# First output-projection chunk inside the attention's last groups, broadcasts behind the scores, and no embedding table: two attention layers in float32

## The reference, cut to what matters

```
x: 2 x 512 x 48 x 48, 8 heads of 64, 2304 tokens per image
layer 0: xn = group_norm(x, 32 groups) * w + b
         q, k, v = qkv_w @ xn + qkv_b
         a = softmax(q k^T / 8) v              (per image and head)
         x = proj_w @ a + proj_b + x
layer 1: emb = 32 rows that depend on the image row h, 32 on its column w
         q, k = [x, emb] @ Wq, [x, emb] @ Wk ; v = x @ Wv
         o = softmax(q k^T / 8) v
         out = o @ Wout + bout + x
```

## Time and profile before

| | us |
|---|---|
| median of 3 runs (4218.84 to 4219.61) | 4218.99 |
| the profiled execution's own time | 4219.53 |
| its span | 4217.8 |
| PE (TensorE) busy | 4099.4, 97% |
| DVE (VectorE) busy | 3278.0, 78% |
| ACT (ScalarE) busy | 2763.7, 66% |
| POOL (GpSimd) busy | 1773.6, 42% |
| waits of PE for ACT before L661, 92 times | 22.6 |

### The profile page before, as it was taken

The page is one execution under the profiler, slowest core; times in us unless marked ns, Lnnn a source line. Parts: engine busy times, 40 slices in busy tenths (PEclk is TensorE's granted clock), DMA queues, the critical chain, the costliest instruction groups (busy, mean ns, idle before and its releaser), DMA issues. The chain is left out here.

```text
span 4217.8 us, 88347 instructions
## 1 busy us (share of the span) xinstructions
PE 4099.4 (97%) x30024; PEld 1901.6 (45%) x30024; DVE 3278.0 (78%) x4032; ACT 2763.7 (66%) x3557; POOL 1773.6 (42%) x572
## 2 busy tenths in 40 slices
PE   7999999999999999998999989999999999999989
PEld 4554344444444444444555544444444444444445
DVE  3111999999999999997322239999999999999962
ACT  1112888888888888886000018888888888888840
POOL 0000455555555555553100005555555555555520
PEclk9999999999999999999999999999999999999999
DMA  4112000101000000011333220101000000000116
GB/s 176 75 75 94 10 27 19 37 13 32 20 28 22 22 23 26 26 49 51 118 102 127 97 95 9 31 20 32 19 28 24 22 22 26 24 21 30 42 47 215
DMA packets 157932, 208.41 MB, mean 49 GB/s; under 512 B 9008, under 2 KB 144304, under 8 KB 156848
## 3 DMA queue, kind: packets, MB, share of 16 engines
q1 hardware_dynamic: 137712, 179.28, 12.9%
q10 hardware_dynamic: 20160, 28.32, 1.8%
HBM read 113.19 MB, written 94.37 MB: 49 GB/s over the span
## 5 line engine op out<-in xcount | busy, mean ns | idle before, releaser
L589 POOL TENSOR_TENSOR prob<-prob,mx 128x1056 f32<-128x1056 f32 x564 | 1752.6, 3107 | 2237.0 <-DVE prob L589 2237.0
L753 ACT ACTIVATE prob<-psum_att 128x768 f32<-128x768 f32 x1728 | 1353.9, 822 | 938.6 <-PE psum_att L684 535.4
L684 PE MATMUL psum_att<-qst,kst 64*128 64x384 f32 x6912 | 1286.2, 504 | 30.3 <-DMA kst<-qk_scratch 17.8
L769 ACT ACTIVATE prob<-prob 128x1152 f32<-128x1152 f32 x1152 | 1292.9, 1175 | 16.5 <-POOL prob L589 14.5
L695 PE MATMUL psum_att<-prob,vst 128*32 128x384 f32 x13824 | 1239.3, 490 | 0.4 <-issue 0.4
L856 DVE TENSOR_TENSOR run<-psum_att,run 128x768 f32<-128x768 f32 x1152 | 1057.8, 947 | 24.3 <-PE psum_att L684 23.1
L589 DVE TENSOR_TENSOR prob<-prob,mx 128x1248 f32<-128x1248 f32 (+1 forms) x576 | 972.1, 1688 | 0.0
L684 PEld LDWEIGHTS psum_att<-qst,kst 64*128 64x128 f32 x6912 | 621.9, 187 | 575.2 <-issue 174.2
L695 PEld LDWEIGHTS psum_att<-prob,vst 128*32 128x32 f32 x13824 | 393.7, 109 | 718.4 <-issue 529.1
L870 DVE TENSOR_TENSOR two_tiles<-prob 128x768 f32<-128x768 f32 x564 | 534.4, 948 | 0.0
L309 PE MATMUL psum<-xc_l,wq 128*128 128x384 f32 x1536 | 504.0, 489 | 9.9 <-DVE qk_l L406 4.8
(11 more groups left out here) (56 smaller groups left out, 1690.9 us busy)
## 6 DMA issues: line engine op xcount, KB each, us to landing
qk_scratch<-qk_l SPq DMA_DIRECT2D x48, 768.0 KB, 3.5
v_scratch<-vo_l SPq DMA_DIRECT2D x24, 768.0 KB, 3.5
qst<-qk_scratch SPq DMA_DIRECT2D x96, 192.0 KB, 2.4
kst<-qk_scratch SPq DMA_DIRECT2D x96, 192.0 KB, 2.4
vst<-v_scratch SPq DMA_DIRECT2D x96, 192.0 KB, 2.5
att_scratch<-ob ACTq DMA_DIRECT2D x96, 192.0 KB, 1.9
attc_l<-att_scratch SPq DMA_DIRECT2D x24, 768.0 KB, 5.4
x_sb<-in_x SPq DMA_DIRECT2D x8, 1152.0 KB, 14.0
```

The lines of the kernel that those rows point to most:

```text
L589: return engine.tensor_tensor(x, x, m, ALU.subtract)
L684: mm = nc.tensor.matmul(psum[:, 2 * k + e, 0:CH], kst[rows, (3 * c + k) * P:(3 * c + k + 1) * P], qst[par][rows, :], start=True, stop=True ...
L753: nc.scalar.activation(prob[par][:, :, s, :], s_banks(k)[:, :, 0:CH], ACT.Copy).then_inc(copied, 1)
L769: nc.scalar.activation(x, x, ACT.Exp, scale=SCALE).then_inc(exp_done, 1)
```

## The change

- The broadcasts of the maximum come behind the scores of group 1, and signal once per pair of banks; VectorE's maxima of group 1 and ScalarE's copies of the maximum wait for them one by one. `spread_den` waits per bank.
- VectorE's share of the shift of group 3 is 304 columns, of the others 208.
- At t = 48, groups 2 and 3, and t = 50, groups 2 and 3, TensorE does one tile each of the next stage's chunk 0 output projection, in banks 0 to 3. In those last bodies the denominators go to banks 4 and 5. The next stage's VectorE reads chunk 0 from there; its TensorE begins with the next thing.
- In layer 1 no table is made: row parts are added as a tile leaves PSUM, column parts in a second, in-place addition in SBUF. TensorE waits for the first addition alone.
- Each tile of x is loaded in two halves, with a semaphore for each.

```diff
-SHIFT_DVE = 208
+XH = 2
+SHIFT_DVE = [208, 208, 208, 304, 208, 208]
+OUT_AHEAD = {(0, 2): (0,), (0, 3): (1,), (2, 2): (2,), (2, 3): (3,)}
@@ first_norm_stage, load_x
-                sp.dma_start(gn["x"][:, c, b * HW:(b + 1) * HW],
-                             x_d[c * P:(c + 1) * P, b * HW:(b + 1) * HW]).then_inc(gn["x_in"][n], 16)
+                for h in range(XH):
+                    tokens = slice(b * HW + h * HW // XH, b * HW + (h + 1) * HW // XH)
+                    sp.dma_start(gn["x"][:, c, tokens], x_d[c * P:(c + 1) * P, tokens]).then_inc(gn["x_in"][n][h], 16)
@@ qkv_stage, TensorE
+            if out_proj:
+                pe.wait_ge(w_in[out_proj["w_at"]], 16)
+                pe.sem_inc(out_mm, CT)
...
-                out_tiles(0, 0)
-                            pe.wait_ge(qk_out, MT * i + m - 3)
+                            pe.wait_ge(qk_read, MT * i + m - 3)
@@ qkv_stage, VectorE
+            def add_cols(i, m):
+                half, mt = divmod(m, CT)
+                dve.wait_ge(qk_read, MT * i + m + 1)
+                nc.vector.tensor_tensor(image(qk[half][:, mt, :]), image(qk[half][:, mt, :]), emb_cols(m), ALU.add)\
+                    .then_inc(qk_out, 1)
...
-                            nc.vector.tensor_tensor(qk[half][:, mt, :], qk_bank(m), emb_of(i, m), ALU.add)\
-                                .then_inc(qk_out, 1)
+                            nc.vector.tensor_tensor(image(qk[half][:, mt, :]), image(qk_bank(m)), emb_rows(i, m),
+                                                    ALU.add).then_inc(qk_read, 1)
+                            if m > 0:
+                                add_cols(i, m - 1)
+                            if m == MT - 1:
+                                add_cols(i, m)
@@ output_stage, TensorE
+                    if is_block(i, 0):
+                        pe.wait_ge(early["out_mm"], CT)
+                        pe.sem_inc(out_mm, CT)
+                        continue
@@ attention_stage, TensorE
-                mm.then_inc(broadcast, 1)
+                    mm.then_inc(broadcast, 1)
...
+                    bank_free(t + 3, DEN_SPREAD_AT, r)
+                    mm = nc.tensor.transpose(spread_part(t, r), dwide[:, r, :], ident)
...
+            def first_out_tiles(tiles):
+                pe.wait_ge(ahead["w_in"], 16)
+                pe.wait_ge(ahead["att_in"], 16)
+                for m in tiles:
+                    w = [ahead["w"][:, c, m * P:(m + 1) * P] for c in range(CT)]
+                    out_projection(nc, psum[:, m, 0:CH], w, ahead["att"]).then_inc(ahead["out_mm"], 1)
...
-                    if c == BROADCAST_AT and not before(t, 1) and live(t - 1):
-                        broadcast_max(t - 1, c)
...
                     if c == TURN_AT and not before(t, 1) and live(t - 1):
                         bank_free(t, c, 2)
                         turn(t - 1)
+                    if c == BROADCAST_AT and not before(t, 1) and live(t - 1):
+                        broadcast_max(t - 1, c)
                     tv, pv, cv = behind(t, par, c, PV_LAG)
                     if live(tv):
                         weigh(tv, pv, cv)
+                    if not live(t) and (t - NB, c) in OUT_AHEAD:
+                        bank_free(t, c, 2)
+                        first_out_tiles(OUT_AHEAD[t - NB, c])
+                    if live(tv):
                         add_keys(tv, pv, cv)
@@ attention_stage, ScalarE, copy_max
-                    act.wait_ge(broadcast, t + 1)
+                act.wait_ge(broadcast, 3 * t + r + 1)
@@ attention_stage, VectorE, maximum
+                if s // 3 == BROADCAST_AT and not before(t, 1):
+                    dve.wait_ge(broadcast, 3 * (t - 1) + s % 3 + 1)
```

More of the change, by code:

```diff
@@ L53, in norm_buffers @@
         gn[name + "_sem"] = ctx.enter_context(nc.semaphore(name))
-    gn["x_in"] = [ctx.enter_context(nc.semaphore(f"x_in{n}")) for n in range(N)]
+    gn["x_in"] = [[ctx.enter_context(nc.semaphore(f"x_in{n}_{h}")) for h in range(XH)] for n in range(N)]
     return gn
@@ L223, in pairs_of_chunks, with image, emb_rows, emb_cols @@
             pair(NCH // 2 - 1, True)
[L225 to L229, removed]
+        def image(x):
+            return x.rearrange("p (h w) -> p h w", w=SIDE)
+        def emb_rows(i, m):
+            return bufs["emb_parts"][:, m, bass.ds(i % JB * (CH // SIDE), CH // SIDE)].unsqueeze(2)\
+                .broadcast_to([P, CH // SIDE, SIDE])
+        def emb_cols(m):
+            return bufs["emb_parts"][:, m, SIDE:2 * SIDE].unsqueeze(1).broadcast_to([P, CH // SIDE, SIDE])
         @block.sync
@@ L511, in _, with attention_stage @@
                 pair(it)
-def attention_stage(nc, name, psum, bufs, qk_d, v_d, att_d, next_loads):
+def attention_stage(nc, name, psum, bufs, qk_d, v_d, att_d, next_loads, ahead):
     with ExitStack() as ctx:
@@ L755, in copy_max @@
             def copy_max(t, par, r):
-                if r == 0:
-                    act.wait_ge(broadcast, t + 1)
-                    if not before(t, 2):
-                        act.wait_ge(dve_shifted, group(t - 2, KC - 1))
-                        act.wait_ge(pool_shifted, group(t - 2, KC - 1))
+                act.wait_ge(broadcast, 3 * t + r + 1)
+                if r == 0 and not before(t, 2):
+                    act.wait_ge(dve_shifted, group(t - 2, KC - 1))
+                    act.wait_ge(pool_shifted, group(t - 2, KC - 1))
                 nc.scalar.activation(mx[par][:, :, r * P:(r + 1) * P], s_banks(r)[:, :, CH:512], ACT.Copy)\
@@ L841, in reduce @@
                 if not before(t, 1):
-                    dve.wait_ge(broadcast, t)
+                    dve.wait_ge(broadcast, 3 * t)
                 nc.vector.tensor_reduce(mcol[:, :, r], s_banks(r)[:, :, CH:512], AX.X, ALU.max).then_inc(reduced, 1)
@@ L876, in shift @@
                 dve.wait_ge(copied, slot(t, 3 * c + 2))
[L877 removed]
+                shift_part(nc.vector, par, c, 0, CH if last(t) else SHIFT_DVE[c]).then_inc(dve_shifted, 1)
             def sum_den(t, k):
@@ L969, in early_loads @@
                      "res": sb_(c1, nc, f"resc0_{stage}", [P, CT, CH])}
-            for signal in ("w_in", "att_in", "res_in"):
+            for signal in ("w_in", "att_in", "res_in", "out_mm"):
                 early[signal] = c1.enter_context(nc.semaphore(f"{signal}_{stage}"))
@@ L974, in early_loads, with attention @@
                            (early["res"][:, :, :], rows(res_d, 0), early["res_in"])]
-        def attention(layer, next_loads):
+        def attention(layer, next_loads, ahead):
             with ExitStack() as c2:
-                psum = c2.enter_context(nc.psum_tensor(f"psum_att{layer}", [P, 8, 512], F32))
                 def two(name, shape, dt=F32):
@@ L991, in attention @@
                         "ones": ones, "ident": ident}
-                attention_stage(nc, f"att{layer}", psum, bufs, qk_d, v_d, att_d, next_loads)
+                attention_stage(nc, f"att{layer}", psum, bufs, qk_d, v_d, att_d, next_loads, ahead)
         def semaphores(c1, stage, n):
@@ L1015, in program @@
             we_in, em_in, wq_in, wv_in = semaphores(c1, "l1", 4)
-            attention(0, [(we[:, :], w1e, we_in), (em[:, :], emb, em_in)] + loads)
+            attention(0, [(we[:, :], w1e, we_in), (em[:, :], emb, em_in)] + loads, early)
             wq = sb_(c1, nc, "wq1", [P, CT, 2 * C])
```

61 lines of the change are left out of this document (24 added, 37 removed).

## The result

Changed kernel: 4226.97 us (4225.29 to 4228.74, 19 runs); kernel before, same chips: 4219.6 us (4218.4 to 4221.3, 19 runs). Ratio 1.0018, 95% interval [1.0011, 1.0024]: slower by 0.18%, where 4175.6 was forecast. The profiled execution's span goes from 4217.8 to 4224.0, +6.3 us; forecast was -43.4, so 49.7 us have to be explained. The steady block's period is 32.48 us (32.26 before, 31.98 forecast), and 86 of them make 43 of the 49.7. Two of the prediction's own signs of being wrong have come: a period above 32.1, and PE waiting elsewhere in the block.

The account below looks back on a forecast made before the run. Bound: a steady-block loop closed by DVE and PE, with three ACT copies between. Gains 24.9 + 1.7 + 1.7 + 10.4 + 3.4 + 1.3 = 43.4 us lead from 4219.5 to 4176.1, median 4175.6; range 4154 to 4205.

Parts of the forecast that it names:

- signs of being wrong: Steady block: wrong if the period is above 32.1 or below 31.8, or if PE waits elsewhere in the block.
- The two idles vanish: Steady block: DVE's two 0.25 us idles, waiting for PE's scores of groups 3 and 4, disappear.
- no stall left, none to spare: Group 1's second and third score tiles: PE reaches each 0.15 us after its copy, just enough for the semaphore.
- The steady sum: Steady block, loop through DVE: 3.71 + 9.74 + 5.29 + 12.67 + 0.57 = 31.98 us, 0.29 less than now.
- the forecast's loop over PE: Steady block: PE between groups 1 and 4 (15.67 becomes 16.34), DVE after it; 31.78 us in all.
- The hold-up: DVE's shift behind the reductions, held up 1.25 us by GpSimd's shift (2.70 against 1.45); 1.1 to 1.25 of it goes.
- PE takes over: Rival, steady block: DVE starts its maximum sooner, period falls to 31.68 to 31.78, time 4154; chance 0.20.
- the hold-up stays: Rival, steady block: GpSimd's time does not go with its columns, period 32.34, time 4210 or 4203; chance 0.16.
- Slower: Rival, group 1: PE holds the first score until the last copy, period 33.38, time 4299; chance 0.05.
- Tails and seams: Attention ends and next stages: each attention ends 2.3 us later; layer 1 gains 10.4, the output stage 3.4.
- The tail gives nothing: Rival, attention tails: the four tiles cost there what they save behind, 7 us of the seams go, 4183; chance 0.09.
- Start: Kernel start: with x in halves only three statistics remain behind the last load; gain 1.3 us, between 0 and 1.4.

Follow-up runs that it names:

- x2: Changed kernel with the denominator's transposes (`turn_den`) moved between group 3's second and third score tiles: 4195.94 us, 0.9948.
- e1: Changed kernel with VectorE's share of the group 3 shift back at 208 columns: 4218.86 us, 0.9998.
- y1: x4 with output tiles 2 and 3 moved from in front of the last denominator to the start of the next stage: 4179.46 us, 0.9903.
- x4: x2 with the shift at 208 columns everywhere: 4187.61 us, 0.9925; run a second time, 4188.42 us.
- x1: e3 with chunk 0's output projection back in its own stage, no tiles ahead: 4198.12 us, 0.9948.
- e3: Changed kernel with both the shift at 208 columns and the broadcasts back ahead of the scores: 4197.63 us, 0.9946.
- x3: e3 with only the last pair of broadcasts put behind the first score tile: 4192.91 us, 0.9937.
- e4: Changed kernel with each pair of broadcasts directly behind its own score tile, 304 columns kept: 4218.08 us, 0.9995.

## Why the prediction was wrong, step by step
**The failed step** is "The two idles vanish since PE, starting group 1 earlier, is 0.2 to 0.3 ahead there". I walked the loop that goes through DVE alone, and the one through PE from group 1 to 4; not the one that leaves PE at the broadcast and returns to it at `turn_den`. In the trace after, it adds up:
- PE from group 3's scores (1510.54) to the next group 1 (1531.24), without idle time: 20.70
- scores and broadcast to DVE's first maximum, 1498.75 to 1501.65: 2.90
- maxima of groups 1 and 2, to 1506.49 + 2.68 = 1509.17: 7.52
- ScalarE's third copy, to 1510.01: 0.84
- `turn_den`, 1510.01 to 1510.54: 0.53

That is 32.49. A sum round a closed loop always gives the period; what shows that this path holds the block is that its links follow on each other without slack, and x2, which takes one link out. DVE's shift of group 3 and its reductions are not in it. They are in a second loop that passes `turn_den` too: from group 3's scores over DVE's work to the reductions (DVE idles only 0.19 and 0.09 in it, for PE), then over ScalarE's copies to the third score tile of group 1. That one is longer by the 0.11 of e1, and it is what the tiles wait for; with 208 columns the first loop is left. The same sum in e1, where the scores take 2.14 and not 2.25, is 32.39 (measured 32.37). The trace of the kernel before was enough to see it. Counted from the start of group 1's scores on PE, `turn_den` was reached after 1504.66 - 1494.96 = 9.70 us and its bank was free after 1504.55 - 1494.96 = 9.59. The new order puts 0.80 of broadcast into the first path, and into the second the difference of the first maximum's start, 2.61 forecast against 1496.20 - 1494.96 = 1.24, so 1.37. From 0.11 early the bank becomes 0.46 late, and with 0.05 from ScalarE to PE that is a wait of 0.51; measured is 0.52. In PE's list of waits it was missing because it was hidden by 0.11.

A second step was too small: "no stall left, none to spare" for the score tiles. PE started group 1 0.10 sooner than forecast and then waited for copies two and three, 0.11 in group 1, and 0.10 for the third tile of group 2. Seen from PE the changed block is 31.67 + 0.59 at `turn_den` + 0.11 + 0.10 = 32.47; the block before was 31.67 + 0.44 + 0.15 = 32.26.

**The steady sum, term by term.** From the first reduction's end to the first maximum, 3.71 forecast, 3.90 measured (PE starts after 1.00 in place of 1.10, but scores take 2.25 in place of 2.13, and from the first broadcast to DVE it takes 0.65 in place of 0.48). The idles before groups 3 and 4, 0 forecast, 0.19 and 0.09 measured. The wider shift 0.57, measured 0.60. Together 31.98 + 0.19 + 0.28 + 0.03 = 32.48. (In the forecast's loop over PE, 15.67 + 0.80 - 0.15 is 16.32 and not 16.34; nothing hangs on it.) Over 86 intervals and the few that fill the pipeline, the attentions' steady parts are 16.5 us longer than before, where 28.3 less was forecast: 44.8 of the 49.7 missed.

**The hold-up** went as forecast: 1.48 in place of 2.70, with GpSimd at 1.86 (1.85 forecast by the rule, 1.41 by scaling). But its 1.2 us came out as DVE idle ahead of the broadcast, as forecast too; in e1, where the shift takes 2.71 again, DVE idles 0.22 there in place of 0.97. The hold-up was a real stall beside the path, and its end is worth nothing unless the path goes through it.

**The rivals.** "PE takes over" and "the hold-up stays" did not happen. "Slower" named a late start of group 1; PE started as forecast. Slower came from a place none of them named.

**Tails and seams.** Last fold of attention 0 to layer 1's chunk 1: forecast -10.4, measured 114.55 to 106.08, -8.5. Attention 1's last fold to the last matmul: forecast -3.4, measured 175.66 to 173.90, -1.8. `wq` landed after 9.04, not 7.9, and the half clock lasted 13.7 us. From the last fold to the next stage's start, tiles 0 and 1 cost nothing in attention 0 (50.17 in y1, 50.16 before) and 0.64 in attention 1 (50.17, 49.53 before); tiles 2 and 3, in front of the last denominator, cost 3.14 and 3.13 (53.31 and 53.30 in x4), near the 3.25 forecast. In the changed kernel all four cost 2.8 and 3.4, where 2.3 was forecast. What was wrong was to pay that for an idle stretch behind it: the table gave 7.4 and the four tiles, as x1 shows, nothing. "The tail gives nothing", at 0.09, was the better case here. Its reason holds in part: from the attention's tail to layer 1's q and k, 13.7 us run at half clock in e3 and 10.2 in x1. That alone is too little; the tiles' own cost in the attention (3.15) and the exposed load of `wq` stand beside it.

**Start.** The first q, k matmul moved from 25.48 to 24.45, -1.0 of 1.3 forecast, but the first scores of attention 0 only from 408.41 to 408.39. The clock rises at 29.39 before and 29.24 after, so an earlier start runs longer at half (the first 64 records take 22.65 and 23.09). The gain of 0.6 that remained was lost behind the load of the keys, for which PE idles 9.03 before and 9.61 after.

**What stays open.** Taking away DVE's wait for the broadcast wasn't tried: the broadcasts write spare columns of the banks that DVE reads then, and no run shows what comes of the two at once. Why it takes 0.65 from the first broadcast to DVE's maximum, and not the 0.48 forecast, isn't explained. x2 and x4 pay 0.2 a block for a break; `turn_den` behind all of group 3's scores wasn't tried.

## What to carry to other kernels
When an order is changed, walk every loop that crosses engines, and list the waits that are satisfied with less slack than the change moves things: here a wait that was met 0.11 us early before came to cost 0.59 us a block, and moving it got 31 us back. A view of waits lists lost time, not slack; the weight loads' view named who came last. Undo parts of a bundle in a square, since parts do not add up: here the order alone cost 21 us, the width alone 51, both together 29. Work moved ahead of a stage pays only where the engine idles already; in front of the last chain it is a straight cost, and best used to fill a load that would be exposed.

## What the runs showed of the hardware
- Putting full-height transposes (128 rows) between score tiles (64 rows) costs TensorE more than the same instructions in one run each: 0.2 us in x2, 0.34 in x3, 0.68 in e4. Against the unbroken order these have 1, 2 and 4 more changes between scores and transposes, so each costs 0.17 to 0.2, however many transposes follow. The Trainium skill says in "TensorEngine Tiling (Array Packing)", section "Key Properties", that changing the tiling mode drains TensorE. The direction agrees; it was not tested whether that is the cause.
- GpSimd's shift of 480 elements beside a VectorE key addition took 1.86 us, more than the 1.41 in proportion to 3.10 for 1056. That fits the forecast's reading, that the first 0.8 of both is waiting for the addition that started before it.
- In the changed kernel the granted clock fell to half (1.2 of 2.4 GHz) at 2002.15, after PE had idled 3.47 us and resumed; the embedding's 3.20 us of matmuls, the gap of 5.55 and 5.45 of the matmuls behind it all ran at half, 13.7 in one stretch. In y1, where the two tiles fill the gap, and in x1 the stretch was 6.8; before there were two of 6.8. At the output stage it was 10.2 in the changed kernel and 6.8 in y1, but e1 (6.8) and e3 (10.2) differ there with the same order of work at that seam.
- A score tile whose copy ends late starts 0.05 us behind it, and its late weight load costs PE up to 0.11 us a group without a row in PE's own view of waits.
